# Four graph layers on one core: an early epilogue in the attention layer, first counts in pieces, tables stored in halves

## The chip, the cores and the metric

The kernel runs on one core of one Trainium2 chip, as one program. The metric is the device time of one execution in microseconds, the median of several; the profile is one further execution, recorded by the hardware profiler.

## The reference

Four layers over 3125 nodes (256 features) and 50,000 edges, each followed by a residual and a layer norm:

```python
edge_index = jnp.stack([src, dst])
x = _layernorm(x + L0(x, edge_index, W, b))          # GCN: degree-weighted neighbour sum, @ W
x = _layernorm(x + L1(x, src, dst, ...))             # GAT, 8 heads of 32
x = _layernorm(x + L2(x, edge_index, ...))           # one attention layer over edges, then 3 SAGE layers
x = _layernorm(x + L3(x, weight, edge_weight1, src, dst, edge_type_16))  # 16 relations
```

What the change touches is the end of L1, the start of L2 and the tables of L3:

```python
# L1                                            # L2, attention
a = e / s[dst]                                  q, k, v = x @ Wq + bq, x @ Wk + bk, x @ Wv + bv
out = segment_sum(feat[src] * a, dst)           logits = sum(q[dst] * k[src], -1) / sqrt(256)
out = leaky_relu(out + gat_bias, 0.01)          attn = segment_softmax(logits, dst)
return h_in + out                               h = relu(segment_sum(attn * v[src], dst) + x @ Ws + bs)
# L3
transformed = einsum('ni,rio->rno', h, weight)  # 16 tables of [nodes, 256]
out = segment_sum(transformed[rel_type, src] * norm, dst)
```

## The kernel before

Nodes stand in 25 tiles of 128 (`P` = 128, `T` = 25, `NP` = 3200); a node tensor is `[128, 25, 256]` in SBUF. The edges are sorted by destination into 416 slots of 128 (`S`). The layers are a row of blocks: each `nc.Block()` holds one program for each engine, and the next block starts when all engines are through with this one. Inside a block the engines run their own programs and wait for each other on semaphores. The order of every program is written out by hand; there is no scheduler.

`attend` (L1852) is the GAT's edge part: 13 chunks of 32 slots. GpSimd gathers source rows, VectorE finds maxima and weights the rows (`weigh`), TensorE sums them by destination in PSUM, and whenever a tile of destinations is complete ScalarE copies its 256 sums into `k.X` and its 8 denominators into `den` (L2188, L2189, semaphore `copied`, two a tile). Its VectorE program ends with the `weigh` of chunk 13.

`project` (L2229) with the name `p3` makes queries, keys, values and the self term. Its VectorE program has `ahead=attended` (L2627): for five tiles it divides by the denominators, adds the bias, applies the leaky ReLU, adds the residual and normalizes (`normalize_tiles`, L2445), which counts `normed`. At `first == 0` it also clamps and inverts all of `den`. It is called for tiles 0 to 4 and 5 to 9 before the first tile's epilogue (L2356, L2357) and then before tiles 5, 10 and 15. ScalarE stages a tile when `normed` says so, TensorE transposes and multiplies it, with two product buffers; VectorE's `work` empties one (`finished`). SyncE first issues eight weight loads (L2254), for which TensorE waits before its first product.

`dense_attention` (L1568) computes the attention over edges as a dense product. The number of edges between two nodes is in `pairs_d` (`NP` by `NP` counts, made earlier). For each tile of 128 destinations: SyncE loads its counts (`pairs`, 1.6 MB, two buffers) and its queries (`q`); GpSimd's `flag` makes `absent`, -BIG where the count is 0; TensorE's `score` makes 3200 scores in 7 chunks of 512 (three PSUM buffers); VectorE's `mask` adds `absent` and takes the maximum, chunk by chunk (L1710); ScalarE exponentiates (L1742); GpSimd's `weigh` multiplies with the counts (L1644); TensorE's `total` transposes the weights (L1672) and multiplies them with the values (L1685); VectorE's `finish` (L1722 to L1725) closes the tile. The order on GpSimd is flag 0, flag 1, weigh 0, flag 2, weigh 1 and so on; the load of tile t+2 waits for `weigh` of tile t.

`sage_layers` follows; then `relation_tables` (L2691) computes 16 products of each tile (8 pairs of relations; ScalarE keeps the even pairs, L2760, VectorE the odd ones, L2783) and SyncE stores them with one DMA of 2 MB a tile (L2716, two buffers of `rows`). `sum_by_destination` (L1762) then gathers rows of these tables (L1786), 416 gathers, and sums them by destination; it begins when the last store has landed.

## Time and profile before

| | |
|---|---|
| time, median of 3 runs | 4144.51 us (4143.07 to 4148.38) |
| profiled execution: time, span | 4129.58 us, 4127.8 us |
| TensorE busy, VectorE, ScalarE, GpSimd | 2950.8, 1739.5, 882.9, 1366.1 us |
| granted TensorE clock, mean | 0.848 |
| chain that ended last | 10% of the span in waits for another core or an unknown queue, 2% on L1822 |

Line numbers are those of the kernel before. Times in a timeline are microseconds from the span's start. The busy shares are means over blocks with different limits; what an edit moves is to be read at its block's end.

### The profile page before, as it was taken

The numbers are of one execution on the slowest core, as the hardware profiler recorded it, in microseconds if no ns is written. First come the engines' busy times: TensorE is split into PE (matmuls) and PEld (weight loads), VectorE is DVE, ScalarE is ACT, GpSimd is POOL, SyncE is SP. The second block draws the span as 40 slices with busy tenths as digits, with TensorE's granted clock in tenths as the row PEclk, the third lists the DMA queues.
The fourth block names the chain that finished last, engine by engine and source line by source line (L and its number), as shares of the span: only waits on it lengthen the run. The fifth ranks groups of instructions, "written<-read, shape, count | busy, mean of one in ns | idle before, by whom it ended". The sixth has DMA issues, their size and how long they took to land. (4 is left out here: it accounts for less than half of the span.)

```text
span 4127.8 us, 44813 instructions
## 1 busy us (share of the span) xinstructions
PE 2950.8 (71%) x13086; PEld 2107.6 (51%) x13087; DVE 1739.5 (42%) x4314; ACT 882.9 (21%) x1237; POOL 1366.1 (33%) x980
## 2 busy tenths in 40 slices
PE   2888689615544545679999998999998998345345
PEld 1455468314433333446666666989893443224233
DVE  5976442526655566743332324444344222111114
ACT  0246543100000000102222224444431221000000
POOL 2122200065545542027667750000000001666664
PEclk9999889756656667889999999999999999666677
DMA  1157874143323321122222217666842444333332
GB/s 55 69 201 254 270 260 152 38 122 95 95 73 103 90 70 38 40 72 73 78 85 77 74 40 264 193 217 196 274 155 102 142 142 135 94 93 92 90 92 87
DMA packets 325253, 504.88 MB, mean 122 GB/s; under 512 B 27225, under 2 KB 238877, under 8 KB 317005
## 3 DMA queue, kind: packets, MB, share of 16 engines
q1 hardware_dynamic: 284477, 391.28, 28.2%
q0 software_dynamic: 40672, 112.31, 9.8%
q8 instruction: 54, 0.88, 0.1%
q14 instruction: 50, 0.41, 0.0%
HBM read 351.56 MB, written 152.75 MB: 122 GB/s over the span
## 5 line engine op out<-in xcount | busy, mean ns | idle before, releaser
L1786 POOL DMA_INDIRECT e7got<-rel_d,rel_i x416 | 394.9, 949 | 1208.4 <-POOLq L2694 1012.5
L1906 POOL DMA_INDIRECT a_got<-feat_d,src_i x416 | 405.2, 974 | 632.8 <-POOLq L2235 286.0
L1420 PE MATMUL s_aggs<-s_blk_r,high 128*128 128x512 f32 (+1 forms) x1050 | 400.6, 382 | 20.0 <-DVE low L1539 19.8
L1420 PE MATMUL s_aggs<-s_blk_r,low 128*128 128x512 f32 (+1 forms) x1050 | 389.1, 371 | 0.0
L1822 PE MATMUL e7sums<-e7got,e7hot 128*128 128x256 f32 x832 | 264.2, 474 | 168.9 <-issue 147.5
L2735 PE MATMUL q_prods<-w,q_xt 128*128 128x512 f32 x800 | 352.7, 599 | 13.4 <-ACT q_xt L2755 13.4
L1638 POOL TENSOR_SCALAR g_absent<-g_pairs 128x3200 bf16<-128x3200 f32 x25 | 274.8, 10992 | 169.9 <-DMA g_pairs<-pairs_d 169.8
L1794 DVE TENSOR_SCALAR e7hot<-iota,dloc,weight 128x128 f32<-128x128 f32 x416 | 116.2, 364 | 479.9 <-DMA g_pairs<-pairs_d 283.3
L1822 PEld LDWEIGHTS e7sums<-e7got,e7hot 128*128 128x128 f32 x832 | 198.1, 243 | 234.2 <-issue 198.8
L1685 PE MATMUL g_sums<-value,g_turned 128*128 128x257 f32 x1250 | 298.0, 382 | 8.6 <-ACT g_turned L1749 8.6
L1663 PE MATMUL g_scores<-key_t,g_q 128*128 128x512 f32 (+1 forms) x700 | 280.0, 556 | 19.2 <-DMA g_q<-query_d 13.1
L826 PE MATMUL u_counts<-u_hot_s,u_hot_d 128*128 128x512 bf16 (+1 forms) x1248 | 221.0, 319 | 48.8 <-DVE u_hot_d L786 36.4
L2735 PEld LDWEIGHTS q_prods<-w,q_xt 128*128 128x128 f32 x800 | 151.0, 191 | 200.5 <-issue 199.8
L2134 PE MATMUL a_sums<-a_got,a_hot 128*128 128x264 f32 x832 | 237.6, 448 | 16.5 <-DVE a_got L2032 11.1
L1685 PEld LDWEIGHTS g_sums<-value,g_turned 128*128 128x128 f32 x1250 | 225.8, 190 | 42.8 <-issue 7.6
L787 DVE TENSOR_SCALAR u_hot_s<-u_places,u_column,u_value 128x1042 bf16<-128x1042 f16 x416 | 229.6, 552 | 0.0
L1481 ACT CAST s_blk_r<-s_blk 128x2560 fp32r<-128x2560 f32 (+1 forms) x105 | 219.0, 2111 | 21.2 <-DMA s_blk<-turned_d 21.2
L1420 PEld LDWEIGHTS s_aggs<-s_blk_r,high 128*128 128x128 f32 x1050 | 198.3, 189 | 46.9 <-ACT s_blk_r L1481 20.2
L1663 PEld LDWEIGHTS g_scores<-key_t,g_q 128*128 128x128 f32 x700 | 129.6, 193 | 170.8 <-issue 131.2
L2134 PEld LDWEIGHTS a_sums<-a_got,a_hot 128*128 128x128 f32 x832 | 181.9, 227 | 64.2 <-issue 28.6
L1420 PEld LDWEIGHTS s_aggs<-s_blk_r,low 128*128 128x128 f32 x1050 | 198.3, 189 | 25.6
L1749 ACT COPY g_turned<-g_flips 128x512 f32<-128x512 f32 (+1 forms) x175 | 92.1, 540 | 460.4 <-PE g_flips L1672 460.4
(427 smaller groups left out, 4498.4 us busy)
## 6 DMA issues: line engine op xcount, KB each, us to landing
s_blk<-turned_d SPq DMA_DIRECT2D x60, 1280.0 KB
rel_d<-q_rows SPq DMA_DIRECT2D x25, 2048.0 KB
s_blk<-turned_d SPq DMA_DIRECT2D x45, 960.0 KB
pairs_d<-u_rows SPq DMA_DIRECT2D x25, 1600.0 KB, 8.1
turned_d<-u_line SPq DMA_DIRECT2D x25, 1600.0 KB, 7.1
g_pairs<-pairs_d SPq DMA_DIRECT2D x25, 1600.0 KB, 6.7
t_blk<-pairs_d SPq DMA_DIRECT2D x20, 1280.0 KB
t_blk<-pairs_d SPq DMA_DIRECT2D x15, 960.0 KB
```

Source lines behind the costliest of these rows:

```text
L787: dve.tensor_scalar(hot_s[:, u, 0:THIRD], places[:], cols(column, j, 1), cols(value, j, 1), ALU.is_equal, ALU.mult).then_inc(made, 1)
L826: return pe.matmul(counts[:, b, 0:taken[b]], hot_d[:, u, :], hot_s[:, u, b * 512:b * 512 + taken[b]], start=first, stop=False)
L1420: last = pe.matmul(aggs[:, idx % 2, half, 0:w], feats[l][part][:, a, half * P:(half + 1) * P], blk_r[:, q % RINGS, a % GA, 0:w], start=a = ...
L1481: act.copy(blk_r[:, q % RINGS, :, 0:w], blk[:, q % RINGS, :, 0:w]).then_inc(rounded, 1)
L1638: pool.tensor_scalar(absent[:, b, :], pairs[:, b, :], 0.0, -BIG, ALU.is_equal, ALU.mult).then_inc(flagged, 1)
L1663: last = pe.matmul(scores[:, n % BUFS, 0:width[n]], q[:, b, a, :], key_t[:, a, n * 512:n * 512 + width[n]], start=a == 0, stop=a == 1)
L1685: last = pe.matmul(sums[:, b, 0:D + 1], turned[:, g % BUFS, a % 4, :], value[:, a, :], start=a == 0, stop=a == T - 1)
L1786: pool.indirect_dma_start(got[:, j % U, :], None, table, bass.IndirectOffsetOnAxis(ap=index[:, j:j + 1], axis=0)).then_inc(arrived[j % U / ...
L1822: return pe.matmul(sums[:, 0:D], hot[:, u, :], got[:, u, :], start=False, stop=False)
L1906: pool.indirect_dma_start(got[:, n % 2, s, :], None, table, bass.IndirectOffsetOnAxis(ap=k.src_i[:, j:j + 1], axis=0)).then_inc(arrived[n ...
L2134: ins = pe.matmul(sums[:, 0:W], hot[:, 4 * g + u, :], got[:, b, 4 * g + u, :], start=False, stop=False)
L2735: last = pe.matmul(prods[:, o % 4, :], xt[:, b, a, :], w[:, a, 2 * o:2 * o + 2, :].rearrange("p r n -> p (r n)"), start=a == 0, stop=a == 1)
```

## The change

Three edits. First, `attend` takes `early`, and its VectorE program, behind the last `weigh`, waits for ten copies and runs `attended` for tiles 0 to 4; `p3` counts five tiles as ready at once and does the rest. `attended` now clamps and inverts `den` for its own five tiles. Second, the dense attention's first queries are loaded first, the first tile's counts come in three pieces of 1024 columns and one of 128, and VectorE makes `absent` for them, piece by piece, ahead of chunks 0, 2, 4 and 6; GpSimd starts with flag 1. Third, the relation tables of a tile are stored in two DMAs of eight relations each.

```diff
+        PIECES = [(0, 1024), (1024, 1024), (2048, 1024), (3072, NP - 3072)]
+        piece_in = [sem(f"piece_in{m}") for m in range(len(PIECES))]
+        first = sem("first")
@@ dense_attention, sync
-            for t in range(3):
+            sp.dma_start(q[:, 0, :, :], query_d[:, :, 0:P]).then_inc(asked[0], 16)
+            for m, (o, n) in enumerate(PIECES):
+                sp.dma_start(pairs[:, 0, o:o + n], pairs_d[0:P, o:o + n]).then_inc(piece_in[m], 16)
+            for t in range(1, 3):
                 fetch(t, t % 2)
@@ dense_attention, gpsimd
-                pool.wait_ge(loaded[b], (t - b) * 8 + 16)
+                pool.wait_ge(loaded[b], (t - b) * 8 + 16 * b)
...
-            flag(0, 0)
             with pool.Fori(0, T // 2) as i:
@@ dense_attention, vector, mask
-                dve.wait_ge(flagged, t + 1)
+                if not isinstance(t, int):
+                    dve.wait_ge(flagged, t)
                 for n in range(CHUNKS):
+                    if isinstance(t, int) and n % 2 == 0:
+                        o, w = PIECES[n // 2]
+                        dve.wait_ge(piece_in[n // 2], 16)
+                        dve.tensor_scalar(absent[:, b, o:o + w], pairs[:, b, o:o + w], 0.0, -BIG, ALU.is_equal, ALU.mult
+                                          ).then_inc(first, 1)
+                        dve.wait_ge(first, n // 2 + 1)
                     dve.wait_ge(scored, t * CHUNKS + n + 1)
@@ attend, vector, behind the loop over chunks
+            dve.wait_ge(copied, 2 * READY)
+            early(dve, Order(dve, estep), 0, READY, normed)
@@
+READY = 5
@@ project, vector
-                ahead(dve, here, 0, 5, normed)
-                ahead(dve, here, 5, 5, normed)
+                dve.sem_inc(normed, READY)
+                ahead(dve, here, READY, 5, normed)
@@ attended
-                if first == 0:
-                    step(dve.tensor_scalar(den[:], den[:], 1e-30, None, ALU.max))
-                    step(dve.reciprocal(den[:], den[:]))
+                step(dve.tensor_scalar(den[:, here, :], den[:, here, :], 1e-30, None, ALU.max))
+                step(dve.reciprocal(den[:, here, :], den[:, here, :]))
...
+            attend(nc, k, feat_d, links_d, er, k.X, den, attended)
@@ relation_tables, sync, store
-                sp.wait_ge(kept_a, t * (RP // 2) + RP // 2 + 2)
-                sp.wait_ge(kept_v, t * (RP // 2) + RP // 2 + 2)
-                sp.dma_start(rel_d[:, bass.ds(t * P, P), :].rearrange("r p f -> p r f"), rows[:, b, :, :]).then_inc(stored[b], 16)
+                for m in range(2):
+                    here = slice(m * R // 2, (m + 1) * R // 2)
+                    sp.wait_ge(kept_a, t * (RP // 2) + (m + 1) * RP // 4 + 2)
+                    sp.wait_ge(kept_v, t * (RP // 2) + (m + 1) * RP // 4 + 2)
+                    sp.dma_start(rel_d[here, bass.ds(t * P, P), :].rearrange("r p f -> p r f"), rows[:, b, here, :]
+                                 ).then_inc(stored[b], 16)
```

The waits of ScalarE and VectorE for `stored` count 32 a tile instead of 16.

## Rows read from the trace of the kernel before

**Rows 1.** The page, part 1: busy us (share of the span) xinstructions.

```profile
PE 2950.8 (71%) x13086; PEld 2107.6 (51%) x13087; DVE 1739.5 (42%) x4314; ACT 882.9 (21%) x1237; POOL 1366.1 (33%) x980
```

**Rows 2.** Timeline, 1650 to 1699: start, us, engine, line, operation, [idle before, releaser].

```profile
1651.99 1.21 DVE L2032 TENSOR_TENSOR a_got<-a_got,a_peaks 128x1024 f32<-128x1024 f32 x1
...
1661.25 0.17 ACT L2189 COPY den<-a_sums 128x8 f32<-128x8 f32 x1
...
1662.61 0.26 DVE L2632 TENSOR_SCALAR den<-den 128x200 f32<-128x200 f32 x1 [9.41 <-PEq L1859]
...
1662.91 1.40 DVE L2633 RECIPROCAL den<-den 128x200 f32<-128x200 f32 x1
...
1675.12 1.70 DVE L2466 TENSOR_SCALAR X<-h,mv,rstd 128x256 f32<-128x256 f32 x5
...
1677.40 3.77 PE L2323 MATMUL p3prods<-wvs,p3xt 128*128 128x512 f32 x4
...
1689.11 0.42 DVE L2656 TENSOR_TENSOR value<-p3prods,bvs 128x256 f32<-128x256 f32 x1
...
1691.65 3.23 PE L2323 MATMUL p3prods<-wvs,p3xt 128*128 128x512 f32 x4 [4.29 <-DVEq L2351]
...
1697.15 1.88 PE L2323 MATMUL p3prods<-wvs,p3xt 128*128 128x512 f32 x4
```

**Rows 3.** Timeline, 1821 to 1879, the dense attention's first tiles.

```profile
1821.39 0.36 SPq L1613 DMA_DIRECT2D g_pairs<-pairs_d  x1
...
1822.49 0.98 SPq L1613 DMA_DIRECT2D g_pairs<-pairs_d  x1
...
1828.26 22.11 POOL L1638 TENSOR_SCALAR g_absent<-g_pairs 128x3200 bf16<-128x3200 f32 x2 [6.65 <-DMA g_pairs<-pairs_d]
...
1828.52 7.21 PE L1663 MATMUL g_scores<-key_t,g_q 128*128 128x512 f32 x12 [13.15 <-DMA g_q<-query_d]
...
1849.60 11.01 PE L1663 MATMUL g_scores<-key_t,g_q 128*128 128x512 f32 x28 [0.71 <-DVE g_tops L1710]
...
1850.02 2.96 ACT L1742 ACTIVATE g_probs<-g_probs,g_top 128x3200 f32<-128x3200 f32 x1 [41.24 <-DVEq L1717]
...
1853.16 6.95 POOL L1644 TENSOR_TENSOR g_probs<-g_probs,g_pairs 128x3200 f32<-128x3200 f32 x1 [2.80 <-ACT g_probs L1742]
...
1866.96 10.99 POOL L1638 TENSOR_SCALAR g_absent<-g_pairs 128x3200 bf16<-128x3200 f32 x1 [6.85 <-DMA g_pairs<-pairs_d]
...
1875.87 2.23 DVE L1725 TENSOR_SCALAR h<-h  x1
```

**Rows 4.** The tile `g_pairs`: ns min/median/max, first and last start; landing of its loads.

```profile
L1638 POOL TENSOR_SCALAR g_absent<-g_pairs x25: 10989/10991/11038, 1828.3 to 2419.6; 128x3200 bf16<-128x3200 f32 x25
...
DMA to landing us min/median/max: 6.5/6.7/9.8
```

**Rows 5.** Timeline, 3477 to 3494, the end of `relation_tables`.

```profile
3477.31 0.69 DVE L2783 COPY q_rows<-q_prods 128x512 f32<-128x512 f32 x1 [2.67 <-PE q_prods L2735]
...
3484.17 0.69 DVE L2783 COPY q_rows<-q_prods 128x512 f32<-128x512 f32 x1 [2.74 <-PE q_prods L2735]
...
3493.99 1.06 POOL L1786 DMA_INDIRECT e7got<-rel_d,rel_i  x1 [1012.54 <-POOLq L2694]
```

**Rows 6.** Windows: stretch, us, busy of five engines, granted clock, DMA share, GB/s.

```profile
1669.00:1671.00 2.00, 0.00 (x0) 0.00 (x0) 1.97 (x3) 0.00 (x0) 0.00 (x0) 0.50 0.03 10
```

**Rows 7.** DMA view: issues, KB each, median us from issue to landing.

```profile
pairs_d<-t_rows SPq DMA_DIRECT2D x1, 200.0 KB, 1.9
...
turned_d<-s_agg_t SPq DMA_DIRECT2D x1, 200.0 KB, 3.4
```

**Rows 8.** Line L1725: ns min/median/max of its instructions.

```profile
L1725 DVE TENSOR_SCALAR h<-h x25: 294/2401/2815, 1875.9 to 2476.9; - x24, 128x256 f32<-128x256 f32 x1
```

**Rows 9.** Groups by line and form: xcount, busy us, mean ns, idle before.

```profile
L463 DVE TENSOR_SCALAR links<-f_same 104x1024 bf16<-104x1024 f32 x1 | 0.7, 693 | 0.0
```

**Rows 10.** Windows at the last table store.

```profile
3486.00:3488.00 2.00, 0.00 (x0) 0.00 (x0) 0.00 (x0) 0.00 (x0) 0.00 (x0) 0.91 0.99 348
```

More of the change, by code:

```diff
@@ L1849, in _, with attend @@
             act.wait_ge(copied, T)
-def attend(nc, k, table, links_d, er, acc, den):
+def attend(nc, k, table, links_d, er, acc, den, early):
     W = D + H
@@ L1897, in attend @@
              "resumed", "made", "weighed", "multiplied", "closed", "full", "copied"))
+        estep, normed = sem("estep"), sem("normed")
         block = c.enter_context(nc.Block())
@@ L2624, in graph_layers @@
                 project(nc, k, "p2", [(k.X, None)], wide, 2 * D + 2 * H, 4, epilogue, stores=[(feat, feat_d)])
-            attend(nc, k, feat_d, links_d, er, k.X, den)
             linear = h
@@ L2713, in store @@
             def store(t, b):
-                sp.wait_ge(kept_a, t * (RP // 2) + RP // 2 + 2)
-                sp.wait_ge(kept_v, t * (RP // 2) + RP // 2 + 2)
-                sp.dma_start(rel_d[:, bass.ds(t * P, P), :].rearrange("r p f -> p r f"), rows[:, b, :, :]).then_inc(stored[b], 16)
+                for m in range(2):
[4 more added lines that the diff above has]
+                                 ).then_inc(stored[b], 16)
             over_tiles(sp, store)
-            sp.wait_ge(stored[0], 16 * (T // 2 + 1))
-            sp.wait_ge(stored[1], 16 * (T // 2))
+            sp.wait_ge(stored[0], 32 * (T // 2 + 1))
+            sp.wait_ge(stored[1], 32 * (T // 2))
         @block.tensor
@@ L2756, in tile @@
                 if reused(t):
-                    act.wait_ge(stored[b], (t - b) * 8)
+                    act.wait_ge(stored[b], (t - b) * 16)
                 for o in range(0, RP, 2):
@@ L2779, in tile @@
                 if reused(t):
-                    dve.wait_ge(stored[b], (t - b) * 8)
+                    dve.wait_ge(stored[b], (t - b) * 16)
                 for o in range(1, RP, 2):
```

## The prediction

> **What bounds the kernel now.** I read the page's first part, then the timeline at the three places that the diff touches, then the windows and the tile and DMA views for what those places wait for. No engine is busy throughout (TensorE 71% [rows 1]): the program is a row of blocks with barriers between them, each bounded by something else, and a microsecond won at a block's bound comes off the end unless the next block waits for something that did not move. So each edit is worth what it moves at its own barrier or first wait.
>
> At the end of `attend` VectorE's last weighting starts at 1651.99 and lasts 1.21 us; then VectorE is idle to 1662.61, where `p3` begins, because the block ends with ScalarE's last copy at 1661.42 [rows 2]. The reader is to see a hole of 9.4 us on VectorE, and a barrier of 1.19 us (1661.42 to 1662.61). Then `p3` is bound by VectorE: it prepares tiles 0 to 4 until 1676.82, tiles 5 to 9 until 1689.1, and TensorE, which has two product buffers, does two tiles (1677.40 to 1687.36, at half clock) and stands 4.29 us until VectorE has emptied one [rows 2].
>
> At the start of the dense attention GpSimd is the bound: two flags in a row, 22.11 us from 1828.26, and the weighting of tile 0 from 1853.16 to 1860.11; TensorE has its second tile of scores ready at 1860.61 [rows 3]. Later tiles run by GpSimd's chain: weighting, load, flag. Its flags follow each other by (2419.6 - 1867.0) / 22 = 25.12 us [rows 3, 4].
>
> At the end of `relation_tables` everybody waits for one store: VectorE's last copy ends at 3484.86, the first gather goes at 3493.99 [rows 5].
>
> **Part 1: tiles 0 to 4 prepared inside `attend`.** The call now costs 1676.82 - 1662.61 = 14.21 us [rows 2]. The two operations on all of `den` (0.26 and 1.40 us for 200 columns) become two on 40 columns: I take a fifth of 1.40 and a fixed part, 0.4, and 0.2 for the other (bounds 0 and 1.40). So the call costs 14.21 - 1.7 + 0.6 = 13.1 us, and each later call takes 0.6 us more than now (1689.1 - 1676.8 = 12.3, plus the two). It starts when VectorE is free, at 1653.2: its new wait is for ten copies of closed tiles, and the graph's tiles 0 to 4 closed long before chunk 13. It ends at 1653.2 + 13.1 = 1666.3, which is 4.9 us after the 1661.42 that ends the block now. Cover is thus 8.2 us of the 13.1. With the same barrier `p3` starts at 1667.5 instead of 1662.6.
>
> In `p3` VectorE does one call instead of two: it is free at 1667.5 + 13.1 = 1680.6, against 1689.1, 8.5 us earlier. What is late next is TensorE: its first product needs the eight weight loads, issued at the block's start, so they move 4.9 us later. In the window from 1669 the DMA share is 0.03 [rows 6], so their bytes were in 6.4 us after the start; with the completion I take 7 (bounds 6.4 and 14.8, since the products began at 1677.40 without waiting). Products then start at 1674.9 and the two tiles, still at the half clock, end 10 us later, 1684.9: the third tile starts then, against 1691.65, 6.8 us earlier. Now TensorE has not idled before it: in the old run the same four products took 3.23 us at 1691.65 and 1.88 at 1697.15 [rows 2], 1.35 us that goes. With what follows in that tile at half clock, 8.4 us in all. The three calls that stand later among the tiles, before 5, 10 and 15, are in the open, since TensorE fills its two buffers and stands: 3 x 0.6 = 1.9 us come back. **Part 1: -6.5 us** (-4.5 to -8.5; if the weights came as late as the row allows, about +1).
>
> **Part 2: the first counts in pieces.** T is 1821.39, the first load's issue. Query tile 0 (128 KB) is now loaded first. No load of that size stands alone in the trace; two stores of 200 KB land in 1.9 and 3.4 us [rows 7], and behind two big loads it took until T+7.1. I take the 1.9 and 0.8 for the issue, T+2.7 (to T+4). TensorE's scores then run from T+2.7 and not from T+7.1 (1828.52). The first 12 products took 7.21 us cold, all 28 take 11.01 warm [rows 3], so about 13.0 from cold: chunks end at about T+6.2, 8.3, 10, 11.8, 13.5, 15.2 and 15.7. A piece of 1024 columns costs VectorE 0.69 us (f32 to bf16, L463 [rows 9]); that is nothing beside chunks of 1.7 us. If that were all, tile 0 would be masked at T+16.3 and not at T+28.
>
> But flag 1 stays on GpSimd and no longer waits behind flag 0: it starts when the counts of tile 1 land. Now that is 9.8 us after an issue at T+1.1, T+10.9 [rows 3, 4]; the bytes ahead of it are the same, the issues more, so I take T+11 (T+10 to T+13). It lasts 10.99 us. And during a flag VectorE's own `tensor_scalar` from SBUF to SBUF does not run: L1725, 256 columns, takes 0.29 us at the least and 2.40 in the median [rows 8]; at 1875.87 it took 2.23 and ended at 1878.10, 0.15 us after the flag that ran from 1866.96 to 1877.95 [rows 3]. The pieces' flags are that kind of instruction. The Trainium skill says it as a rule (SBUF — State Buffer, section "Who interferes with whom"): VectorE in a two-port mode and GpSimd share a port pair, and the one that comes second "fully blocks". This trace agrees, with the 2.23 us.
>
> Piece 1 is flagged after chunk 1's mask, at T+9.1: just in time. Piece 2 comes after chunk 3's mask, at T+12.5, and stands until T+22; behind it on VectorE's queue are the masks of chunks 4, 5 and 6 and piece 3. They end at T+24.5, the exponential (2.96 us) at T+28, and GpSimd's weighting (6.95) at T+35.2, against T+38.7 (1860.11). TensorE waits for the mask of chunk 6 for its next scores, has gone cold, and has them at T+24.6+13.0 = T+37.6, against T+39.2. If the counts land so late that piece 2 slips through, piece 3 is the one that stands, and the sum is the same within 0.5 us. If piece 1 is caught too (the query at T+4, or the counts at T+10), TensorE also stands before its own chunk 5 and all is gone: 0 us. After the first tile, GpSimd's lead of 3.5 us is what later tiles can use, TensorE's 1.6 what they have at once. **Part 2: -2 us** (0 to -3.5; -9.5 without the standing).
>
> **Part 3: tables in halves.** Of the last tile, the first eight relations are kept when VectorE's copy at 3477.31 ends, 3478.0, 6.9 us before the rest [rows 5]. A tile is 2.1 MB; at 348 GB/s that is 6.0 us [rows 10], a half 3.0. The first half is through by 3482, so after 3484.9 only 3.0 us of transfer are left instead of 6.0. SyncE issues 50 stores instead of 25, at some 0.4 us in a tile of 14.7 us, hidden; the buffers come free no later than now. **Part 3: -3 us** (-2 to -3.3).
>
> **Sum.** 6.5 + 2 + 3 = 11.5 us. The profiled execution has a span of 4127.8 and a time of 4129.58 us and would become 4118.1; the timed runs stand 15 us above it (median 4144.51), and I take the difference off their median: 4133.0.
>
> **The rivals.** (a) VectorE's pieces do not stand: f32 to bf16 might not need what GpSimd holds. For: nothing in the trace shows this very form beside a flag. Against: 1024 columns in 0.69 us is half of what a copy of 512 from PSUM takes for each column, 0.69 us for all [rows 5], so it reads and writes SBUF twice as fast as that one does PSUM, as L1725's 0.29 us for 256 does. Then GpSimd's flag 1 ends at T+22, weighting at T+29.2, TensorE's scores at T+28.5: -9.5 us, in all -19, time 4125.5.
> (b) Less of it: piece 1 is caught as well (part 2 gives 0), or the weights land 9 us after the start (part 1 gives 4.5), or the second half of the last store keeps a fixed cost (part 3 gives 2). Two of the three give about -7: 4137.5.
> (c) The other side: TensorE falls to half clock in every dense tile. Its place is the wait for the weighting before each tile's transposes; the point is an idle of about 4.3 us, which is what stood before the slow products at 1691.65 [rows 2]. Price: 2.1 us (13.0 - 10.9) in each of 24 tiles, 50 us, against 11.5 won: 4183. Against it: GpSimd's chain comes out ahead of TensorE, not behind it, so no idle should grow. Any slower result from causes that I do not see is counted here.
> (d) The change does what it says nowhere: the early call would have to wait for the block's end. Then `p3` starts 13 us later, wins nothing and pays the 1.9; parts 2 and 3 remain, -3: 4141. Its chance is in (b).
>
> **How the numbers follow.** Forecast 0.5, (a) 0.2, (b) with (d) 0.25, (c) 0.05. A change under 0.2% (8.3 us) can't be told from none here. The forecast's own range is 4129 to 4136, all faster but for its last tenth; (a) is faster; (b) lies astride 4136.2, a third of it faster, the rest the same. So faster 0.45 + 0.2 + 0.09 = 0.74, same 0.21, slower 0.05. The range has (a) with part 1 at its best and a median 3 us low on one side, 4120, and (b) on the other, 4139.
>
> **What would show it.** Part 1: VectorE goes on at 1653 without a hole, the block ends about 4.9 us later, first products 7 us after the start, no idle of 4.3 us before the third tile, later calls 0.6 us longer. Part 2: a piece's flag with a duration of 7 to 10 us, ending with GpSimd's flag 1; if all four take 0.7 us, (a) is right. Part 3: last store to first gather 6.1 us instead of 9.1. Wrong would be a first product later than 1680, or a dense period away from 25.1 us.

## The result, and the profile after

The median of 7 runs is 4132.55 us (4126.69 to 4140.65), against 4147.8 us (4141.78 to 4155.36) for 7 runs of the kernel before on the same chip. The ratio is 0.9966, with an interval of 0.9953 to 0.9979, so the change takes off 14.1 us (8.7 to 19.5). Forecast were 11.5 us, 4133. The profiled execution after took 4131.62 us with a span of 4129.8, two us more than that of before. That of before stands 18.2 us under the median of these timed runs (4129.58), that of after 0.9, so the gain is not to be seen in the two spans; it has to be read stage by stage. The stages, each measured from a first to a last instruction that both kernels have (us):

| stage | before | after |
|---|---|---|
| start to `attend`'s first `weigh` | 938.1 | 944.2 |
| first to last `weigh` of `attend` | 713.9 | 714.9 |
| last `weigh` to `p3`'s first weight load | 10.5 | 15.2 |
| that load to the dense attention's first load (T) | 158.9 | 146.9 |
| T to tile 0's transposes | 39.05 | 39.13 |
| T to the last `weigh` of the dense attention | 632.0 | 632.1 |
| T to `sage_layers`' first block load | 662.6 | 663.7 |
| that load to the first product of `relation_tables` | 629.4 | 630.9 |
| from there to the end of VectorE's last copy | 371.6 | 371.8 |
| end of the last copy to the first gather | 9.1 | 6.1 |
| first gather to the end | 633.8 | 636.2 |

Rows five and six lie within row seven. Rows four and ten are the gain, 15.0 us; row three takes 4.7 back. The others add 12.4 us, 10 of it in the first, the eighth and the last row (6.1, 1.5 and 2.4 us), which the change doesn't touch. A stage varies by so much from one execution to the next (the first to the last `weigh` by 19 us, below); the timed runs average over that, one profile doesn't.

**Part 1** as it answers to [rows 2]. The timeline of the kernel after (start, us, engine, line, operation, [idle before, releaser]):

```profile
1659.05 1.21 DVE L2047 TENSOR_TENSOR a_got<-a_got,a_peaks 128x1024 f32<-128x1024 f32 x1
1660.18 0.18 DVE L2651 TENSOR_SCALAR den<-den 128x40 f32<-128x40 f32 x1
1660.39 0.40 DVE L2652 RECIPROCAL den<-den 128x40 f32<-128x40 f32 x1
...
1669.60 0.17 ACT L2206 COPY den<-a_sums 128x8 f32<-128x8 f32 x1
...
1671.61 1.71 DVE L2487 TENSOR_SCALAR X<-h,mv,rstd 128x256 f32<-128x256 f32 x5
1674.22 0.39 SPq L2275 DMA_DIRECT2D wqk<-in_L_gnn_Wq  x1
1674.46 0.18 DVE L2651 TENSOR_SCALAR den<-den 128x40 f32<-128x40 f32 x1 [1.15 <-PEq L1873]
...
1681.76 0.66 PE L2334 MATMUL p3flips<-ident,p3xs 128*128 128x128 f32 x2 [5.90 <-DMA bvs<-in_L_gnn_bs]
...
1682.21 3.20 PE L2344 MATMUL p3prods<-wvs,p3xt 128*128 128x512 f32 x4
...
1690.97 1.88 PE L2344 MATMUL p3prods<-wvs,p3xt 128*128 128x512 f32 x4
```

VectorE goes on at 1660.18 without the hole. ScalarE's last copy ends at 1669.77, and VectorE's call at 1673.32: the block now waits for VectorE, and 1.15 us of barrier follow. The products begin 7.75 us after the block's first VectorE instruction, released by the last of the weights, at a granted clock of 0.59. The third tile's run at 1690.97 without an idle and at a granted clock of 1.00, 1.88 us for four instead of 3.23.

**Part 2** as it answers to [rows 3]. The same timeline at the dense attention's start; T is 1821.15:

```profile
1823.76 13.19 PE L1669 MATMUL g_scores<-key_t,g_q 128*128 128x512 f32 x28 [8.62 <-DMA g_q<-query_d]
...
1826.15 0.69 DVE L1718 TENSOR_SCALAR g_absent<-g_pairs 128x1024 bf16<-128x1024 f32 x1 [8.54 <-DMA g_pairs<-pairs_d]
...
1830.45 0.69 DVE L1718 TENSOR_SCALAR g_absent<-g_pairs 128x1024 bf16<-128x1024 f32 x1
...
1833.00 11.04 POOL L1645 TENSOR_SCALAR g_absent<-g_pairs 128x3200 bf16<-128x3200 f32 x1 [11.62 <-DMA g_pairs<-pairs_d]
...
1833.88 10.71 DVE L1718 TENSOR_SCALAR g_absent<-g_pairs 128x1024 bf16<-128x1024 f32 x1
...
1846.82 13.62 PE L1669 MATMUL g_scores<-key_t,g_q 128*128 128x512 f32 x28 [9.87 <-DVE g_tops L1723]
1847.24 2.96 ACT L1755 ACTIVATE g_probs<-g_probs,g_top 128x3200 f32<-128x3200 f32 x1 [38.70 <-DVEq L1730]
...
1850.39 6.94 POOL L1651 TENSOR_TENSOR g_probs<-g_probs,g_pairs 128x3200 f32<-128x3200 f32 x1 [6.35 <-ACT g_probs L1755]
```

Piece 0's and piece 1's flags take 0.69 us. Piece 2's takes 10.71 and ends at 1844.59, half a microsecond behind GpSimd's flag 1 (1833.00 + 11.04 = 1844.04). TensorE stands 9.87 us and makes the next scores in 13.62 us, at a granted clock of 0.81. The transposes come at T+39.13, where they came at T+39.05.

GpSimd has tile 0 weighted at T+36.2, where it had it at T+38.7: a lead of 2.5 us. GpSimd and ScalarE, same view:

```profile
1864.59 10.99 POOL L1645 TENSOR_SCALAR g_absent<-g_pairs 128x3200 bf16<-128x3200 f32 x1 [7.26 <-DMA g_pairs<-pairs_d]
1875.80 6.99 POOL L1651 TENSOR_TENSOR g_probs<-g_probs,g_pairs 128x3200 f32<-128x3200 f32 x1 [0.22 <-ACT g_probs L1755]
...
1872.65 2.96 ACT L1755 ACTIVATE g_probs<-g_probs,g_top 128x3200 f32<-128x3200 f32 x1
```

Here `weigh` of tile 1 waits for the exponential (1875.61), with flag 2 just done (1875.58); from the next tile on it waits for its flag again. The lead is not gone with that. `weigh` ends ahead of its tile's transposes by 2.95, 2.42, 1.91, 1.45, 1.18, 0.80, 0.78 and 0.55 us in tiles 0 to 7, and by less than 0.5 from there on, as in every tile of the kernel before. It is used up tile by tile, because TensorE does a tile in 24.96 us there and GpSimd's chain takes 25.3.

What the lead is worth at the stage's end hangs on GpSimd's chain, which is a wait for the counts to land, a flag of 11.0 us and a weighting of 6.95 us, 23 times over. Its waits for the landing (us in total, times, longest) behind tile 0's `weigh`, before and after:

```profile
POOL g_absent L1638 <- DMA g_pairs<-pairs_d: 163.1, 23, 7.4
POOL g_absent L1645 <- DMA g_pairs<-pairs_d: 165.5, 23, 7.5
```

They took 2.4 us more in the execution after, and that is why both kernels' last `weigh` comes at T+632. The landings scatter by as much without the change: in the four profiles with the old start (the kernel before and, below, e1_early, e3_halves and e9_before_again) the last `weigh` stands at T+632.0, 632.5, 634.3 and 633.2, in the three with the new one (the kernel after, e2_pieces and e6a_early_in_gap) at T+632.1, 632.1 and 630.3. The means are 1.5 us apart, a difference that this scatter tells neither from 0 nor from 2.

**Part 3** as it answers to [rows 5]:

```profile
3480.71 7.25 SPq L2739 DMA_DIRECT2D rel_d<-q_rows  x2
...
3486.81 0.69 DVE L2807 COPY q_rows<-q_prods 128x512 f32<-128x512 f32 x1 [2.74 <-PE q_prods L2759]
...
3493.57 1.04 POOL L1799 DMA_INDIRECT e7got<-rel_d,rel_i  x1 [1010.76 <-POOLq L2715]
```

Two stores go out, the first one while the last products are made; from the end of the last copy (3487.50) to the first gather are 6.1 us instead of 9.1.

### The profile page after: what moved, and what is told of

It is laid out like the page before. It is cut to its first block and busy times, and to the rows that moved or that the text cites. A ratio compares the mean times of both kernels' runs of the same rounds, so it can differ in the third digit from the quotient of the medians.

```text
span 4129.8 us, 44872 instructions
## 1 busy us (share of the span) xinstructions
PE 2936.4 (71%) x13021; PEld 2105.1 (51%) x13087; DVE 1747.4 (42%) x4326; ACT 883.8 (21%) x1237; POOL 1358.2 (33%) x979
## 5 line engine op out<-in xcount | busy, mean ns | idle before, releaser
L1645 POOL TENSOR_SCALAR g_absent<-g_pairs 128x3200 bf16<-128x3200 f32 x24 | 263.9, 10994 | 177.1 <-DMA g_pairs<-pairs_d 177.1
L826 PE MATMUL u_counts<-u_hot_s,u_hot_d 128*128 128x512 bf16 (+1 forms) x1184 | 210.1, 316 | 58.7 <-DVE u_hot_d L786 40.6
```

The costliest lines, as they stand in the source:

```text
L826: return pe.matmul(counts[:, b, 0:taken[b]], hot_d[:, u, :], hot_s[:, u, b * 512:b * 512 + taken[b]], start=first, stop=False)
L1645: pool.tensor_scalar(absent[:, b, :], pairs[:, b, :], 0.0, -BIG, ALU.is_equal, ALU.mult).then_inc(flagged, 1)
```

## The experiments

Eleven runs were made, of eight changed kernels and, on a third chip, of two of them and the kernel before again (the labels that end in `again`). Those told of together ran on one chip, if nothing else is said. The kernel before has its own median on each: 4121.04 us (29 runs) on the first, 3792.85 (9) on the second, 4148.01 (11) on the third.

### The three parts alone

Each kernel is the kernel before with one part of the change, its lines as in the diff above.

```diff
# e1_early: attend(..., den, attended), READY, attended's own five tiles of den
# e2_pieces: PIECES, queries first, VectorE's flags, GpSimd from flag 1
# e3_halves: two stores a tile
```

> Only part 1 (early call in attend, three later calls 0.6 us longer). Theory A (each part is worth what its own stage shows; the early call has 8 us of cover): last weighting to the dense attention's first load 160.9 us instead of 168.2, about -7 us, timed 0.998 of before. Rival B (what the timed runs gained beyond the three stages, 14 against 9 to 10 us, belongs to part 1): -11 us or more, and some stage far from p3 shorter too. Dense attention and the last store as in the kernel before (first load to first transposes 39.0 us; last copy to first gather 9.1 us).

> Only part 2. Theory A (the flags of pieces 2 and 3 stand behind GpSimd's flag of tile 1): one piece flag of 10 to 11 us that ends with GpSimd's flag, first load to first transposes 39.1 us as before, timed 1.000 (0 us, up to +1.5). Rival B (the standing was luck of this one trace): pieces of 0.7 us, first transposes at 29 to 30 us, timed 0.9977, -9.5 us.

> Only part 3. Theory A (half of the last store's 6.0 us of transfer has gone before): last copy to first gather 6.1 us instead of 9.1, timed -3 us, 0.9993. Rival B (a DMA of 1 MB is no faster to land than one of 2 MB, since a fixed time dominates): 8 to 9 us, no change.

Timed, with 12 runs each: e1_early 4113.79, ratio 0.9974 (0.9962 to 0.9987), 10.7 us less; e2_pieces 4116.22, ratio 0.9983 (0.9971 to 0.9994), 7 us less; e3_halves 4117.46, ratio 0.9999 (0.9984 to 1.0015), 0.4 us less, with an interval of 6.6 us less to 6.2 more. The interval of e1_early, 5 to 16 us less, holds both the 7 and the 11 us of its expectations; its stages decide. The 1.000 expected of e2_pieces lies outside its interval.

The stages say: e1_early 15.2 us from the last `weigh` to the first weight load and 162.6 to T, where before has 169.4: 6.8 us won, nothing elsewhere. e3_halves 6.1 us from the last copy to the first gather, 3.1 won. e2_pieces: the transposes at T+39.37, the last `weigh` at T+632.1, nothing to be told from the scatter above, and from `attend`'s last `weigh` to T, which it leaves alone, 2.9 us more than before. Its piece stood again. The tile `g_absent` of e2_pieces (ns min/median/max, first and last start):

```profile
L1645 POOL TENSOR_SCALAR g_absent<-g_pairs x24: 10992/10992/11040, 1823.7 to 2410.1; 128x3200 bf16<-128x3200 f32 x24
L1718 DVE TENSOR_SCALAR g_absent<-g_pairs x4: 224/690/10553, 1816.8 to 1836.7; 128x1024 bf16<-128x1024 f32 x3, 128x128 bf16<-128x128 f32 x1
```

So the parts by their stages are 6.8, about 0 (to 1.5) and 3.1, and their timed differences 10.7, 7 and 0. They don't agree by part. What lies between is larger than any part: the first to the last `weigh` of `attend`, untouched but for the wait behind it, took 713.9 us in the profile of before, 706.7, 700.3 and 700.2 us in these three, and 719.2 in the next kernel, on their chip too. A part of 3 us is told by its stage and not by a median. The 7 us timed for e2_pieces (2.5 to 12) have no stage that shows them; they are left unexplained. Its profiled execution, 4123.43 us, was the slowest of its twelve.

### All four flags ahead of flag 1

The flags no longer wait for their masks, so that they are through before tile 1's counts land.

```diff
-                for n in range(CHUNKS):
-                    if isinstance(t, int) and n % 2 == 0:
-                        o, w = PIECES[n // 2]
-                        dve.wait_ge(piece_in[n // 2], 16)
+                if isinstance(t, int):
+                    for m, (o, w) in enumerate(PIECES):
+                        dve.wait_ge(piece_in[m], 16)
                         dve.tensor_scalar(absent[:, b, o:o + w], ...).then_inc(first, 1)
+                    dve.wait_ge(first, len(PIECES))
+                for n in range(CHUNKS):
```

> The changed kernel, but VectorE flags all four pieces as they land, ahead of the first mask, so none is left when GpSimd starts flag 1. Theory A (standing is the whole reason that part 2 gave nothing): four flags of at most 0.7 us, GpSimd weights tile 0 right behind flag 1, first load to first transposes 30 us instead of 39.1, and the lead lasts through the stage: about -9 us against the changed kernel, -19 to -23 against the kernel before. Rival B (the stage's length is set by something that does not move, such as the load-flag-weighting chain or TensorE's period, which swallow a lead): first transposes at 30 us, but last weighting 632 us after the first load as now, timed as the changed kernel.

Timed 4097.1 us (6 runs), ratio 0.994 (0.9921 to 0.996) on the first chip. Its flags in the view of `g_absent`, and its second tile's scores in the timeline:

```profile
L1717 DVE TENSOR_SCALAR g_absent<-g_pairs x4: 222/694/694, 1827.4 to 1830.6; 128x1024 bf16<-128x1024 f32 x3, 128x128 bf16<-128x128 f32 x1
```

```profile
1838.68 5.42 PE L1669 MATMUL g_scores<-key_t,g_q 128*128 128x512 f32 x12 [0.71 <-DVE g_tops L1723]
1846.36 7.52 PE L1669 MATMUL g_scores<-key_t,g_q 128*128 128x512 f32 x16 [2.26 <-DVE g_tops L1723]
1853.71 1.04 PE L1678 MATMUL g_flips<-ident,g_probs 128*128 128x128 f32 x8
```

Here the standing is taken away, by another order, and all else of part 2 is there: no flag over 0.694 us, tile 0 weighted at T+30.2, 6.0 us earlier than in the kernel after, the transposes at T+31.6, 7.5 earlier. The last `weigh` comes at T+624.4, 7.7 earlier: GpSimd's 6.0 us, kept over 24 tiles, and waits for the landings that were 1.6 us shorter (163.9 us). So piece 2's standing costs about 6 us here. The 24.7 us timed (16 to 33) are more than the stages hold (7 + 7.7 + 3, some 18); the profiled execution, 4120.08 us, was the slowest of its six. On the third chip the same kernel was run again beside the kernel before:

> The kernel before, once more, for its stages on the chip of the two that stand beside it. The theory (the attention layer waits 11 us of every chunk for its gathers where these are slow, about 714 us for the layer, and for VectorE where they are fast, about 510 us): on a chip with a time near 4120 the layer takes 700 to 719 us and VectorE's idle before a chunk's first scan is 11 to 21 us; on one near 3790 it takes 500 to 515 us with 0 to 4 us of idle. The rival, that the two kinds of chip differ in the clock: the dense stage, 632.0 us from the first load to the last weigh, would differ by as large a share as the attention layer (28%); by the theory it stays within 628 to 636.

> All four piece flags ahead of GpSimd's flag 1, timed beside the version with the calls inside the chunks. Theory: its dense gain does not hang on the chip: transposes at T+31.6 and the last weigh at T+624.4 within 1 us, on either chip, and the time 18 us under before by its stages (the call inside the layer may give back 3 to 12 of it where VectorE has no idle time there: 6 to 15 us under before on a chip near 3790). Rival: the 24.7 us that its runs showed is its real size: then it is over 22 under before again.

e9_flags_first_again took 4129.39 us (6 runs), ratio 0.9956 (0.994 to 0.9972): 18.3 us less, the 18 of its stages and not the 24.7. Its transposes stood at T+29.83, 1.8 us before the T+31.6 that was expected within 1 us, the last `weigh` at T+623.3; the profile of before there has T+39.04 and T+633.2. Tile 0 was weighted at T+29.7, 9.0 us before it was in the kernel before, and the last `weigh` is 9.9 us earlier. In the second tile's scores TensorE's clock did not fall; first this kernel, then e9_inside_again (below), which has the same start:

```profile
1834.72 5.42 PE L1669 MATMUL g_scores<-key_t,g_q 128*128 128x512 f32 x12 [0.71 <-DVE g_tops L1723]
1841.86 5.86 PE L1669 MATMUL g_scores<-key_t,g_q 128*128 128x512 f32 x16 [1.72 <-DVE g_tops L1723]
```

```profile
1815.97 5.86 PE L1669 MATMUL g_scores<-key_t,g_q 128*128 128x512 f32 x16 [2.54 <-DVE g_tops L1723]
```

The last sixteen products took 5.86 us after 1.72 us of idle and after 2.54 us, both at a granted clock of 1.00, but 7.52 us after 2.26 us in e4_flags_first, at 0.78. So the length of this idle alone does not decide whether the clock falls.

### GpSimd's flag later, or shorter

e8_flag1_later leaves VectorE's order as in the change and has GpSimd wait for the four pieces. e5_short_flag halves GpSimd's flags: it leaves out the edges of the right half of the columns, which stay at -BIG.

```diff
# e8_flag1_later, gpsimd, ahead of flag 1
+            pool.wait_ge(first, len(PIECES))
# e5_short_flag, gpsimd
+            pool.memset(absent[:, :, NP // 2:NP], -BIG).then_inc(cleared, 1)
-                pool.tensor_scalar(absent[:, b, :], pairs[:, b, :], 0.0, -BIG, ALU.is_equal, ALU.mult).then_inc(flagged, 1)
+                pool.tensor_scalar(absent[:, b, 0:NP // 2], pairs[:, b, 0:NP // 2], 0.0, -BIG, ALU.is_equal, ALU.mult).then_inc(flagged, 1)
```

> The changed kernel, but GpSimd waits with its flag of tile 1 until VectorE has flagged the last piece of tile 0. Theory A (only one of the two engines can go: if GpSimd goes second, VectorE's flags take 0.7 us and GpSimd's whole chain comes 4 to 5 us later): the last piece's flag at 15 to 16 us after the first load, flag 1 from 16 to 27, weighting to 34.5, transposes at 34 to 35 us; -4.5 us against the changed kernel. Rival B (the flags stand because of something else than GpSimd's instruction, such as the landing of the pieces): a piece's flag of 10 us again.

> The changed kernel, where GpSimd's flag does only the left half of the columns of each tile after the first (the right half stays at -BIG: those edges are left out of the sums). Each flag takes 5.5 us instead of 11.0. It asks what sets the dense attention's 25.1 us a tile. Theory A (after the result: TensorE's own period does; GpSimd's load, flag and weighting is just as long by coincidence, and swallows no lead): last weighting of the stage still 590 us or more after tile 0's transposes (593 in the changed kernel). Rival B (the step of the prediction: GpSimd's chain sets it, TensorE could do a tile in 24.9): 588 or less, some 0.2 us a tile. In both the flag of piece 2 stands only until the shorter flag ends, about 5 us, and tile 0's transposes come at 33 to 34 us instead of 39.1.

One run each on the second chip, 3775.61 and 3774.92 us. e8_flag1_later: no flag over 0.695 us, the transposes at T+37.35, not at T+34 to 35. Most of the miss is TensorE's clock. Its timeline:

```profile
1585.07 5.42 PE L1670 MATMUL g_scores<-key_t,g_q 128*128 128x512 f32 x12 [1.15 <-DVE g_tops L1724]
1596.98 8.59 PE L1670 MATMUL g_scores<-key_t,g_q 128*128 128x512 f32 x16 [6.50 <-DVE g_tops L1724]
1605.40 1.04 PE L1679 MATMUL g_flips<-ident,g_probs 128*128 128x128 f32 x8
```

After 6.50 us of idle sixteen products take 8.59 us, at a granted clock of 0.68, 2.7 more than the 5.86 above; tile 0 was weighted by T+34.9, and without the 2.7 us the transposes would have come then. The last `weigh` stands at T+629.3, 2.7 before the kernel after's, but 0.9 before that of e6a_early_in_gap (below), which has the change's dense program and ran on this chip. On this chip tile 0 is weighted at T+36.1 with the change's order (e6a_early_in_gap), at T+34.9 with GpSimd held back, and at T+29.7 with VectorE's flags moved (e6_inside). So of the two ways to take the standing away, moving VectorE's flags wins GpSimd's chain 6.4 us and holding GpSimd's flag wins it 1.2.

e5_short_flag: GpSimd's flag takes 5.59 us instead of 10.99, in all 24 tiles. Piece 2's flag stands until it ends, 5.01 us, and the transposes come at T+32.8. From the first transposes to the last `weigh` it needs 589.7 us, between the 590 or more of the one theory and the 588 or less of the other. The kernel before and the kernel after need 592.9 and 593.0, e6a_early_in_gap and e8_flag1_later on this chip 591.2 and 592.0, all other profiles up to 595.2. What decides is what `weigh` waits for; the idle time ahead of it in the kernel before (L1644), after (L1651) and here (L1654), with the number of waits:

```profile
  ACT g_probs L1742: 18.5, 2
  ACT g_probs L1755: 22.3, 3
  ACT g_probs L1759: 144.3, 25
```

With the short flag every `weigh` waits for the exponential, so TensorE's scores lead, and the transposes of tiles 0 to 23 come every 24.96 us. With the full flag `weigh` waits for the exponential in the first and the last tile, and once more in the kernel after; in the others GpSimd's own chain leads, and the transposes come every 25.10 us in the kernel before. So GpSimd's chain is the bound, as the prediction had it, and TensorE's own period lies only 0.15 us under it. A lead of GpSimd reaches TensorE at 0.15 us or a little more a tile, some 3.5 us over the stage at most.

### The early call elsewhere

e6a_early_in_gap moves the early call from behind the last `weigh` to behind the ninth chunk's (`n == 8`). e6_inside has the four flags first and makes twenty tiles inside `attend`, five each behind the `weigh` of `n` = 6, 8, 10 and 12; the last of these is the one at the layer's end.

```diff
# e6a_early_in_gap, attend, vector, at the end of the loop over chunks
+                if n == 8:
+                    dve.wait_ge(copied, 2 * READY)
+                    early(dve, Order(dve, estep), 0, READY, normed)
# e6_inside, the flags as in e4_flags_first, and
+                if n in CALLS:
+                    dve.wait_ge(copied, 2 * CALLS[n] + 10)
+                    early(dve, ahead_order, CALLS[n], 5, normed)
-READY = 5
+READY = 20
+CALLS = {6: 0, 8: 5, 10: 10, 12: 15}
-                    if t % 5 == 0 and 5 <= t <= 15:
-                        ahead(dve, here, t + 5, 5, normed)
```

> The changed kernel with the early call moved from the end of the attention layer to the gap after its ninth chunk, where VectorE idles 14 to 20 us for the gathers. Theory A (at the end only 8.2 of its 13.1 us are covered; in a gap all are): last weighting to the first weight load 10.5 us as in the kernel before instead of 15.1, so -4.7 us, and the attention layer no longer than its usual 700 to 719 us. Rival B (VectorE's instructions hold up the gathers or the chunk behind it): chunks 9 and 10 grow by some 10 us and the gain is lost.

> A version after the findings: all four pieces flagged first, and the calls for tiles 0 to 19 inside the attention layer, three in gaps (after chunks 7, 9 and 11) and the one for tiles 15 to 19 at its end, only tiles 20 to 24 in p3. Theory A (p3 lost 13 us less two tiles in flight at each of its three later calls; the gaps cover them in full): first weight load to the dense attention's first load 108 us instead of 147, so -38 us against the variant with the flags first, timed about 0.985 of the kernel before. Rival B (VectorE's work in the gaps holds up the chunks): the attention layer grows by 10 us or more for each call and p3's gain is given back: 0.992 or above.

On the second chip, e6a_early_in_gap took 3781.55 us (one run), e6_inside 3764.45 us (5 runs), ratio 0.9919 (0.9905 to 0.9932), 31 us less where 56 were expected. Behind `attend` both did about what was expected: from the last `weigh` to the first load of weights 11.9 us in e6a_early_in_gap (10.5 expected, 15.2 in e8_flag1_later), and from that load to T 108.3 us in e6_inside (147.5). The first won 3.8 us by that up to T. But the layer grew: its first to last `weigh` took 516.8 and 540.6 us, against 509.5 in e8_flag1_later and 513.4 in e5_short_flag. The expectation was made from the trace on another chip, where VectorE is idle for 10 to 22 us ahead of nearly each chunk. On the second chip it is idle there for 5 us at most once the layer runs. The windows of the layer, of e8_flag1_later and e6_inside (columns: stretch, us, busy of PE, PEld, DVE, ACT and POOL, granted clock, DMA share, GB/s):

```profile
895.90:1405.40 509.50, 333.89 (x1701) 262.87 (x1701) 424.10 (x681) 47.86 (x107) 358.17 (x366) 0.73 0.41 118
```

```profile
903.10:1443.70 540.60, 333.48 (x1694) 261.64 (x1693) 461.04 (x779) 47.84 (x107) 364.93 (x366) 0.72 0.39 112
```

VectorE has 37 us more to do and the layer is 27 to 31 longer. That the gap is a matter of the chip could then be tested:

> The three further calls inside the attention layer. Theory: they cost what the layer's idle time of VectorE does not cover. On a chip near 4120 (11 to 21 us of idle in each of 13 chunks) the layer stays at 700 to 719 us and the whole of 39 us saved behind it remains: 55 to 60 us under before. On a chip near 3790 the layer grows by 27 to 31 us and 25 to 37 us under before remain. Rival (the calls also hold the gathers' starts back, whatever the idle time): the layer grows by 12 us a call on either chip, and on one near 4120 no more than 35 us remain.

On the third chip the same kernel took 4090.43 us (4 runs), ratio 0.986 (0.9839 to 0.9881): 58 us less (49 to 67), 55 to 60 expected. The windows of the layer there, of e9_before_again and e9_inside_again:

```profile
935.80:1658.90 723.10, 341.95 (x1699) 268.69 (x1699) 423.00 (x681) 47.85 (x107) 343.05 (x352) 0.65 0.28 81
```

```profile
940.10:1668.80 728.70, 339.48 (x1702) 267.48 (x1701) 461.30 (x780) 47.84 (x107) 348.32 (x352) 0.66 0.28 80
```

The reader is to see 423 us of VectorE's work in 723.1 us here and 424 in 509.5 there, with 81 and 118 GB/s moved. Here 38 us more work make the layer 5.6 us longer, less than it varies by; there 37 us made it 27 to 31 longer. So the rival, a growth on either chip, falls. Where the work went shows in the view of a chunk's scan, first e9_before_again, then e9_inside_again:

```profile
L1966 DVE TENSOR_TENSOR_SCAN a_turned<-a_penx,a_turned x13: 2282/2283/2283, 915.5 to 1624.9; 32x1024 f32<-32x1024 bf16 x13
its engine sat idle before it (us, times) until:
  remote: 217.6, 12
```

```profile
L1982 DVE TENSOR_TENSOR_SCAN a_turned<-a_penx,a_turned x13: 2282/2283/2283, 920.9 to 1634.8; 32x1024 f32<-32x1024 bf16 x13
its engine sat idle before it (us, times) until:
  remote: 164.4, 10
```

Twelve waits of 18 us each became ten of 16. In e8_flag1_later on the second chip the same view has 43.8 us in 7 waits, for TensorE, 25.3 of it ahead of the first chunk, and none of the kind `remote`.

The expectations call these waits a wait for the gathers. The trace does not show that. `remote` is a release that the profile can't put down to anything, and in e9_before_again's fourth chunk the rows were there long before it: the last gather was issued at 1038.99 and the last landing of them is at 1041.8, and the transposes of its rows, whose end the scan waits for, are recorded 23 us ahead of the scan. First that chunk, then the same one in e8_flag1_later:

```profile
1060.32 1.04 PE L2092 MATMUL a_turned<-ident,a_got 128*32 128x128 f32 x8
1084.23 2.28 DVE L1966 TENSOR_TENSOR_SCAN a_turned<-a_penx,a_turned 32x1024 f32<-32x1024 bf16 x1 [20.35 <-remote]
```

```profile
1000.32 1.86 PE L2110 MATMUL a_turned<-ident,a_got 128*32 128x128 f32 x8 [5.90 <-DMA a_got<-feat_d,src_i]
1002.32 2.28 DVE L1982 TENSOR_TENSOR_SCAN a_turned<-a_penx,a_turned 32x1024 f32<-32x1024 bf16 x1 [4.28 <-PE a_turned L2110]
```

On the second chip the scan follows the transposes by 0.1 us, on the third by 22.9. What holds it back stays open. What the runs show is that the wait is there on the first and the third chip and not on the second, and that VectorE's work fits into it.

The expectation on the clock holds: the dense attention's stage is 633.2 us here, and e6_inside's transposes and last `weigh` stand at T+29.88 and T+624.4 on the second chip, T+29.89 and T+623.8 on the third. So the chips differ in the stages with gathers and not in the others; their clock is no explanation. The layer of the kernel before took 723.1 us where 700 to 719 were expected; its scatter is wider than I had it.

e6_inside has the shortest time of the versions run, on both chips that it ran on. On the third it is 39 us faster than e9_flags_first_again (4129.39 us).

## Why the prediction was right

The sum was 11.5 us and 14.1 were timed, within the interval. By its steps:

- **Part 1, call inside `attend`** (predicted: layer's end 4.9 us later, products 7 us after the start, third tile 8.4 us earlier with the clock, -6.5). Right. The gap grew from 10.5 to 15.2 us, the products began 7.75 us after the start, and T came 7.3 us earlier seen from the last `weigh`, 6.8 in e1_early. The invert of `den` on 40 columns took 0.40 us and the clamp 0.18, 0.58 where 0.6 was taken; a call took 13.13 us (13.1), each later one 0.66 more than before (0.6). The third tile's products took 1.88 us, as the rows of full clock had it. One slip is in the sum: 1667.5 + 7 is 1674.5 and not 1674.9, so that its own terms give -6.9. Its sign of being wrong, a first product later than 1680, came in the letter (1682.21) and not in the matter: seen from the last `weigh` it came after 23.2 us, where 22.9 were forecast, and all of this execution stood 7.1 us later by then.
- **Part 2, start.** Query and counts landed as estimated: the first product at T+2.6 (T+2.7), flag 1 at T+11.85 (T+11), `weigh` of tile 0 ended at T+36.2 (T+35.2).
- **Part 2, standing.** Right, and it decides: piece 2's flag stood 10.71 us until GpSimd's flag was through, as [rows 8] had it for a much smaller instruction. The Trainium skill says of this (SBUF — State Buffer, "Who interferes with whom") that of GpSimd and a VectorE in a two-port mode the one that comes second on their shared port pair is fully blocked. This case's traces agree, with 10.71, 10.55 and 5.0 us behind flags of 11.04, 11.04 and 5.6 us; and with the order turned, no flag of VectorE took over 0.70 us. Rival (a) falls with it, and its price is borne out where the standing is gone: 9.5 us forecast, 9.9 between the last `weigh` of e9_before_again and of e9_flags_first_again.
- **Part 2, worth: right in its bound, wrong in one term, and its size is not measured.** That GpSimd's chain bounds the stage, read from the flags' distance of 25.12 us [rows 3, 4], is borne out by e5_short_flag, where only the shorter flag makes every `weigh` wait for the exponential. "GpSimd's lead of 3.5 us" was 2.5. "TensorE's 1.6 what they have at once" did not come at all: its second tile's scores began at T+25.67 and took 13.62 us, where T+24.6 and 13.0 were taken, and the transposes came at T+39.13 instead of T+37.6. The 13.0 was too small by its own rows: 7.21 us for twelve cold products and sixteen twenty-eighths of 11.01 are 13.5. In this pair of profiles the part gave 0 for the -2 of the forecast (its own range was 0 to -3.5), because the landings took 2.4 us more; over seven profiles it gave 1.5, which the scatter does not tell from either.
- **Part 3** (-3). Right, 3.0 and 3.1 us by the stage; the issues were hidden. The timed runs of e3_halves, with an interval 13 us wide, can't show it.
- **The rest.** By stages the change is worth 7.3 + 0 + 3.0 = 10.3 us in this pair, less 1.1 to `sage_layers`' first load. There the last tile's first eight sums ran at a granted clock of 0.50 in this execution (3.77 us, where before has 2.65), from a `weigh` that came at the same T+632; e1_early, with the same call, has 2.51 us. The timed 14.1 hold that within their interval, 8.7 to 19.5. That the median of 4132.55 lies within 0.5 us of the forecast 4133 is luck in part: the seven timed runs of before had a median 3.3 us above the three that the forecast was taken off, and the timed difference holds 3.8 us that no stage shows.
- **Rival (b)**: of its terms, part 2's 0 came in this pair, but not by its cause; piece 1's flag took 0.69 us. The weights landed 7.75 us after the start and not 9, and the last store won 3.0 us and not 2.
- **Rival (c)**, a half clock in each dense tile, did not come: the stage to the last `weigh` is the same within 0.1 us, and its flags are 25.2 us apart. As a mechanism in one tile it is real, in e8_flag1_later after 6.50 us of idle.
- **Rival (d)** falls: the call ran at 1660.18, while the layer's last copies were still to come.

## What to carry to other kernels

An even distance between one engine's instructions doesn't make it the bound: here two chains have periods of 25.10 and 24.96 us, and only shortening one of them told which leads. A lead in the chain that bounds the stage is kept to its end, but it reaches the other engine only at the difference of the periods, and a few us of scatter in the loads can hide it in one pair of profiles. Work that VectorE does between SBUF tensors beside a long elementwise instruction of GpSimd belongs ahead of it in time; here that order alone was worth 6 us, and holding GpSimd back only 1.2. Before work is put into an engine's idle time, ask whether that idle time is there on every chip: 38 us of VectorE's work made the layer 5.6 us longer, within its scatter, on a chip where VectorE idled, and 27 to 31 us longer on one where it didn't.

## What the runs showed of the hardware

- Chips differ by 8 to 9% on this kernel (4121 and 4148 us against 3793), most of it in the two stages that gather rows: `attend`'s first to last `weigh` took 700 to 723 us on the first and third chip and 509.5 and 513.4 on the second, first to last of the last gathers 588 to 596 and 520 us. Some 30 to 40 us more lie ahead of `attend`'s first `weigh` (934 to 944 against 896 to 903). The other stages agree: 629.4 to 630.9 us for `sage_layers`, 370.9 to 371.8 for the tables, and 591.2 to 595.2 from the dense attention's first transposes to its last `weigh` with a full flag, as wide on one chip as between them.
- In `attend` VectorE idles 10 to 22 us ahead of nearly each chunk on the first and third chip, on a release that the profile can't name and after the gathered rows were there; not on the second.
- TensorE's clock after an idle stretch, sixteen products each, in the first or second tile of the dense attention in five kernels: 5.86 us after 1.72 us and after 2.54 us of idle (granted 1.00), 7.52 after 2.26 (0.78), 8.61 after 4.54 in the first tile of the kernel before (0.68), 8.59 after 6.50 (0.68).
- An instruction of VectorE that stood ended 0.55 us behind the end of GpSimd's (1844.59 and 1844.04), and the trace books the standing as its duration, 10.71 us for 0.69 of work: a duration far from the form's median is how to find it.
